# A CIN recommendation tower on one core: group 0 worked in two parts, its rows and every later group's wrapped rows reloaded from DRAM, plain W2 features kept in the rows' memory

## The reference

```python
def _cin_layer(X0, Xi, W, b):            # X0 (512, 39, 16), Xi (512, k, 16)
    Wr = W.reshape(H, 39, Xi.shape[1])   # H = 128
    return einsum('hjk,bjd,bkd->bhd', Wr, X0, Xi) + b[None, :, None]
Xi = X0 = e                              # the gathered rows
for W, b in ((W0, b0), (W1, b1), (W2, b2)):
    Xi = _cin_layer(X0, Xi, W, b)
    res.append(Xi.sum(axis=2))           # z: (512, 3 * 128)
h = concatenate([z, dense_ctx], axis=1)  # (512, 400)
h = maximum(h @ W_top1 + b_top1, 0)      # 512
h = maximum(h @ W_top2 + b_top2, 0)      # 256
y = h @ W_top3                           # (512, 1)
```

## Time and profile before

| | |
|---|---|
| median of 3 runs | 664.6 us (663.94 to 665.81) |
| profiled execution, its own time | 664.95 us |
| its span | 663.1 us |
| mean granted TensorE clock | 0.992 |
| busy: PE, DVE, ACT, POOL | 95%, 82%, 77%, 56% of the span |
| group 0's T starts | 44.9 us |
| group 1's T starts | 79.3 us |
| last T chunk of group 15 | 605.5 us |

### The profile page before, as it was taken

One profiled execution on the slowest core, in us unless ns is written; L12 is line 12 of the kernel. 1 busy time (PEld: TensorE's weight loads), 2 busy tenths in 40 slices (PEclk: granted clock), 3 DMA queues, 4 the chain that ended last, 5 costly groups with the idle time before them and its releaser, 6 DMA issues.

```text
span 663.1 us, 12298 instructions
## 1 busy us (share of the span) xinstructions
PE 633.2 (95%) x2577; PEld 470.6 (71%) x2577; DVE 544.1 (82%) x1526; ACT 510.0 (77%) x1745; POOL 372.6 (56%) x312
## 2 busy tenths in 40 slices
PE   0589999999999999999999999999999999998998
PEld 0247777777777777777777777777777777785574
DVE  0348789888989898989899888989898989899492
ACT  2138878888788878887888888788878887896394
POOL 6888557675657576766756665756575222224000
PEclk9799999999999999999999999999999999999999
DMA  6357687767677787767677767677787765566100
GB/s 226 55 101 162 121 181 147 159 135 161 127 161 140 155 161 155 149 143 145 145 142 144 157 135 162 126 162 133 154 162 155 153 149 129 136 125 208 33 0 1
DMA packets 62138, 91.18 MB, mean 137 GB/s; under 512 B 34695, under 2 KB 38708, under 8 KB 61863
## 3 DMA queue, kind: packets, MB, share of 16 engines
q0 software_dynamic: 14192, 51.02, 43.0%
q1 hardware_dynamic: 47926, 39.95, 21.9%
HBM read 10.69 MB, written 1.28 MB: 18 GB/s over the span
## 4 chain that ended last, share of the span: by engine, by line
PE 87%; POOL 4%; DMA 4%; DVE 2%; issue 1%; SPq 1%; ACT 0%; DVEq 0%; POOLq 0%
PE t_bank L503 21%; PE t_bank L504 20%; PE t_bank L505 20%; PE x_bank L461 8%; PE small_bank L488 5%; POOL emb L371 4%; PE t_bank L571 2%; PE x_bank L457 2%; PE x_bank L456 2%; PE x_bank L459 2%; DMA shared<-rep 1%; DVE prod L806 1%; DMA prod<-in_w 1%; PE t_bank L605 1%; PE t_bank L602 1%
## 5 line engine op out<-in xcount | busy, mean ns | idle before, releaser
L682 ACT ACTIVATE prod<-t_bank,x0t 128x128 f32<-128x128 f32 x1472 | 416.6, 385 | 70.0 <-PE t_bank L505 63.8
L806 DVE SCALAR_TENSOR_TENSOR prod<-t_bank,x0t,prod 128x128 f32<-128x128 f32 x1024 | 286.6, 341 | 49.3 <-PE t_bank L505 48.8
L503 PE MATMUL t_bank<-w_hi,x_hi 128*128 128x512 f32 (+1 forms) x640 | 288.9, 451 | 1.4 <-DVE x_lo L795 1.1
L504 PE MATMUL t_bank<-w_lo,x_hi 128*128 128x512 f32 (+1 forms) x640 | 247.2, 386 | 0.0
L505 PE MATMUL t_bank<-w_hi,x_lo 128*128 128x512 f32 (+1 forms) x640 | 246.7, 385 | 0.0
L371 POOL DMA_INDIRECT emb<-in_table,idx x160 | 215.7, 1348 | 48.5 <-issue 47.9
L381 POOL TENSOR_TENSOR diag<-x0t,mask 128x320 f32<-128x320 f32 x64 | 85.0, 1328 | 182.0 <-PE small_bank L488 104.9
L503 PEld LDWEIGHTS t_bank<-w_hi,x_hi 128*128 128x128 f32 x640 | 120.2, 188 | 46.1 <-issue 16.4
L504 PEld LDWEIGHTS t_bank<-w_lo,x_hi 128*128 128x128 f32 x640 | 120.5, 188 | 37.8 <-issue 14.4
L505 PEld LDWEIGHTS t_bank<-w_hi,x_lo 128*128 128x128 f32 x640 | 120.1, 188 | 23.7
L838 DVE TENSOR_TENSOR prod<-prod 128x768 f32<-128x768 f32 x189 | 113.7, 601 | 0.2
(11 more groups left out here) (104 smaller groups left out, 382.1 us busy)
## 6 DMA issues: line engine op xcount, KB each, us to landing
prod<-prod POOLq DMA_DIRECT2D x63, 768.0 KB, 6.4
shared<-rep SPq DMA_DIRECT2D x96, 234.0 KB
shared<-rep SPq DMA_DIRECT2D x48, 78.0 KB
emb<-in_table,idx POOLq DMA_INDIRECT x160
G<-in_w SPq DMA_DIRECT2D x1, 2496.0 KB
rep<-rep SPq DMA_DIRECT2D x28, 78.0 KB
rep<-emb_scratch SPq DMA_DIRECT2D x20, 78.0 KB
prod<-in_w SPq DMA_DIRECT2D x1, 1536.0 KB, 8.1
```

The lines of the kernel that those rows point to most:

```text
L503: pe.matmul(acc, hi, w1_hi[:, cols], start=True, stop=False)
L504: pe.matmul(acc, hi, w1_lo[:, cols], start=False, stop=False)
L682: last = act.activation(prod[:, s, SLOT[c] + u, :], t_bank[c % T_BANKS][:, u * H:(u + 1) * H], ACT.Copy, scale=x0t[:, s, j:j + 1])
L806: last = dve.scalar_tensor_tensor(unit, t_bank[c % T_BANKS][:, u * H:(u + 1) * H], x0t[:, s, j:j + 1], unit, ALU.mult, ALU.add)
```

## The change

- **Group 0 in two parts** of 256 columns. Each part has its own ids, loaded folded so that 5 gathers of 126 or 124 rows bring it in (`gather_part`); the second part's gathers follow the first's. SP stores and loads each part (`store_part`, `load_part`). Pairs of a part are 256 columns wide, formed in `prod` memory. The even second factors of the first part are issued by ACT, the odd ones by SP. T starts when the first part's x1 is split. The second part's pairs, products and x1 run inside tiles 0 and 1 of group 0's T, at p = 7 to 18.
- **Group 1's pairs** move to late in group 0: DVE forms them at p = 24 to 33, PE multiplies at p = 27 to 36, all seven as plain f32 matmuls with no split; X0 is transposed after p = 20, x1 follows at p = 37 and 38.
- **Gathers.** POOL issues both parts and group 1 before its first diagonal; group 2's ten are issued in group 0, five after the first diagonal and five after the first fold, then nine of group 3.
- **Wrapped rows.** `load_x0` makes all four loads from DRAM for every group; `copy_x0` goes. All four stand between b5 and b6 in `factors`.
- **W1** is loaded and split in four pieces; ACT's second and third splits wait for the first part's gathers. Small loads are spread: some to ACT's queue, four to the end of the loop.
- **Tail.** 31 features are split, 8 plain. The plain ones' W2 columns are loaded in one DMA into `rep`, once group 15's rows have been used. Three plain products stand before the G product of tile 62 and one before that of tile 63.

The core of the diff:

```diff
-SPLIT_J = 30
+SPLIT_J = 31
+W2_LOADS = [(0, SLOTS), (SLOTS, SPLIT_J)]
+W1_PIECES = [(0, 12), (12, 20), (20, 28), (28, F)]
+PART_X0T_AT = 8
+PART_FORM_AT = [7 + b for b in range(BLOCKS)]
+PART_PAIR_AT = [10 + b for b in range(BLOCKS)]
+PART_X1_AT = (1, 7)
+PART_LO_AT = 18
+FIRST_X0T_AT = 20
+FIRST_FORM_AT = [24, 25, 27, 28, 30, 31, 33]
+FIRST_PAIR_AT = [27, 28, 30, 31, 33, 34, 36]
+FIRST_X1_AT = (3, 7)
+FIRST_LO_AT = 38
+FIRST_GATHERS = [(0, 5), (5, 10), (0, 4), (4, 9)]
+FIRST_INDEX_TILE = 2
...
-            def load_x0(g, half, rows):
-
-                sp.wait_ge(emb_stored, (g + 1) * 16)
+            def load_x0(g, half):
+
+                sp.wait_ge(emb_stored, g * 16)
                 src = emb_rows[bass.ds(g * SLOT_ROWS, GROUP_ROWS), :].rearrange("(b f) d -> f b d", f=F)
-                for row in rows:
+                for row in range(0, REP_ROWS, F):
...
-            def copy_x0(g, half):
...
                     if then_x0 and b == LOAD_BEHIND:
-                        load_x0(g + 1, 1 - half, [0])
+                        load_x0(g + 1, 1 - half)
...
+            store_part(0)
+            load_w1(3)
+            load_part(0)
+            factors_of_part(0)
+            store_part(1)
+            load_part(1)
+            factors_of_part(1)
+
+            store_rows(1, 1)
+            load_x0(1, 1)
+            factors(1, 1, then_x0=True)
...
+            sp.wait_ge(x0t_mm, GROUPS)
+            sp.dma_start(w2_plain, w2[:, SPLIT_J * H:F * H]).then_inc(w2_plain_loaded, 16)
...
+            for part in range(PARTS):
+                gather_part(part)
+            pool.wait_ge(ids_loaded, 16 * 2)
+            index(1, 1)
+            for i in range(GATHERS):
+                gather(i, 1)
...
+            def gather_part(part):
+
+                n = FOLDS * PART_SIZE[part]
+                pool.wait_ge(part_ids_loaded[part], 16 * PART_IDS_LOADS)
+                pool.tensor_tensor(part_idx[0:n, part, :], part_ids[0:n, part, :], part_at[0:n, part, :],
+                                   ALU.add).then_inc(part_index_ready, 1)
...
                 i = b // 2
-                if b % 2:
+                if isinstance(g, int) and g == 1:
+                    pe.matmul(x1_bank[:, :], w_sum[:, b, :], pairs_of(b),
+                              start=b == 0, stop=b == BLOCKS - 1).then_inc(pair_mm, 1)
...
-            for loaded in w2_loaded:
-                pe.wait_ge(loaded, 16)
+            pe.wait_ge(w2_plain_loaded, 16)
             early, late = slice(0, EARLY_COLS), slice(EARLY_COLS, B)
-            for j in range(SPLIT_J, SPLIT_J + EARLY_J // 2):
+            for j in range(SPLIT_J, SPLIT_J + EARLY_J - 1):
                 plain_z2(j, early, start=j == SPLIT_J)
...
+            split_w1_hi(0)
+            act.wait_ge(part_gathered[0], 16 * PART_GATHERS)
+            act.dma_start(prod[:, 0, B1_SLOT, :], b1.to_broadcast([P, H])).then_inc(loop_loaded, 16)
+            act.dma_start(mask[:, :], sample_mask).then_inc(loop_loaded, 16)
+            for i in range(1, W1_EARLY):
+                split_w1_hi(i)
...
+            for b in range(2, BLOCKS, 2):
+                act.dma_start(part_second_at(0, b), rep[b:b + PAIRS, 0, part_cols(0)]).then_inc(part_second[b - 1], 16)
+            for s in range(PART_TILES):
+                copy_x0t(0, s, first=True)
+            split_w1_hi(W1_EARLY)
+            part_x1_hi()
```

More of the change, by code:

```diff
@@ L268, in _, with load_part_ids, load_w1 @@
         def _(sp):
+            def load_part_ids(part):
+                begin, n = PART_BEGIN[part], PART_SIZE[part]
+                for fold in range(FOLDS):
+                    sp.dma_start(part_ids[fold * n:(fold + 1) * n, part, :],
+                                 ids[begin:begin + n, fold * PART_GATHERS:(fold + 1) * PART_GATHERS]).then_inc(part_ids_loaded[part], 16)
+            def load_w1(i):
+                cols = slice(W1_PIECES[i][0] * H, W1_PIECES[i][1] * H)
+                sp.dma_start(w1_raw[:, cols], w1[:, cols]).then_inc(w1_loaded[i], 16)
@@ L322, in factors @@
                     if then_x0 and b == LOAD_BEHIND:
-                        load_x0(g + 1, 1 - half, [0])
-            for g in range(2):
-                store_rows(g, g)
-                load_x0(g, g, range(0, REP_ROWS, F))
-                if g == 0:
-                    factors(0, 0)
-            with sp.Fori(1, GROUPS - 2, 2) as odd:
-                for g, half in ((odd, 1), (odd + 1, 0)):
-                    factors(g, half, then_x0=True)
-                    copy_x0(g + 1, 1 - half)
+                        load_x0(g + 1, 1 - half)
@@ new lines, in _ @@
+            store_part(0)
[8 more added lines that the diff above has]
+            factors(1, 1, then_x0=True)
+            with sp.Fori(2, GROUPS - 2, 2) as even:
+                for g, half in ((even, 0), (even + 1, 1)):
+                    factors(g, half, then_x0=True)
+            sp.dma_start(bias[:, 1:2], b2).then_inc(tail_loaded, 16)
@@ L335, in _ @@
+            sp.dma_start(bias[:, 2:2 + M1], top_b1).then_inc(tail_loaded, 16)
+            sp.dma_start(bias[:, 2 + M1:], top_b2).then_inc(tail_loaded, 16)
+            sp.dma_start(w3[:, :], top3).then_inc(tail_loaded, 16)
+            factors(GROUPS - 2, 0, then_x0=True)
             factors(GROUPS - 1, 1)
@@ L409, in group @@
                     t = g * TILES_PER_GROUP + s
-                    if early and s == INDEX_TILE:
+                    if early and s == (FIRST_INDEX_TILE if first else INDEX_TILE):
                         index(g + AHEAD + 1, 1 - half)
@@ L417, in group @@
                         fold((s - 1) % TILES_PER_GROUP)
-                    if gathers and s < INDEX_TILE:
+                    if first:
+                        for i in range(*FIRST_GATHERS[s]):
+                            gather(i, half if s < FIRST_INDEX_TILE else 1 - half)
+                    elif gathers and s < INDEX_TILE:
                         for i in range(GATHERS_EARLY, GATHERS):
                             gather(i, half)
-                    if early and s >= INDEX_TILE:
+                    if early and not first and s >= INDEX_TILE:
                         for i in range(3 * (s - INDEX_TILE), 3 * (s - INDEX_TILE) + 3):
@@ L497, in t_chunk @@
                     pe.wait_ge(x0t_ready, then_x0t * TILES_PER_GROUP)
+                if first_tile and c in W1_CHUNKS:
+                    pe.wait_ge(w_split_lo, W1_CHUNKS.index(c) + 1)
                 if not (first_tile and c < T_BANKS):
@@ L584, in _ @@
             g_multiply(TILES - 1, 2)
-            for j in range(SPLIT_J + EARLY_J // 2 + 1, SPLIT_J + EARLY_J):
-                plain_z2(j, early)
             pe.wait_ge(g_copied, TILES)
```

350 lines of the change are left out of this document (246 added, 104 removed).

## The result

The changed kernel takes 667.99 us (median of 10, 666.7 to 669.6) against 664.76 us for the kernel before (10, 662.4 to 665.8) on the same chip, a ratio of 1.0053 with the interval 1.0038 to 1.0069. It is 3.2 us slower; the forecast was 661.5 and faster. The profiled execution has a span of 667.4 us in place of 663.1, 4.3 more; its own time, 669.23 us, is 1.2 above the median of its ten, so it stands at their slow end.

The account below looks back on a forecast made before the run. PE, 87% of the span, was taken as the bound, with gains only before T, in the first group and in the tail. 664.95 - 1.0 (head) - 2.4 (tail) = 661.55, given as 661.5; own range 659 to 664.5, overall 653.5 to 668.

Parts of the forecast that it names:

- T of group 0: Head: with 5 gathers in place of 10 in the first part, T starts at 31.0, 13.9 us earlier.
- The sum over POOL: POOL in group 0: gathers, index instructions, diagonals, fold and DVE holds add to 59.8; group 2's rows landed at 61.4.
- the held gather: Head: the second part's fourth gather waits on POOL for DVE's W1 split to end, 3.6 us lost.
- rival (a): Group 0: DVE holds no gather, group 2's rows land at 55.8; 656 us, or 652 with quick landings; chance 0.28.
- Later groups: Fourteen groups swap three copies for more reloads; b6 comes about 0.8 us later, cost taken as zero.
- its cover: Later groups: slack before a later b6 costs time, DVE's 1 us and PE's 3.8.
- rival (c): Every later group: b6 lands after PE's use; 0.5 us each is 7 us, total 668.5; chance 0.08.
- The tail: End of kernel: W2's columns already there, tile 62's G product at 613.4, 2.0 earlier; 2.4 us gained in all.
- rival (d): Tail does nothing, say because the clock falls and W2 was not awaited; 664, no change; chance 0.07.
- The last line of the sum: Whole kernel: 664.95 - 1.0 - 2.4 = 661.55 against the profiled execution, 0.35 above the median; stated as 661.5.
- From those rows to group 1: SP's store, reloads and b6 after group 2's gathers: group 1 starts at 78.3, leaving 1.0 of the head's 13.9 us.
- Rival (b): Group 0: store falls behind tile 1's fold, group 1 at 84.1, clock costs 1 to 2 us; 668 us; chance 0.12.

Follow-up runs that it names:

- Experiment 7: Group 0's folds cut to 16 of 128 rows: in the changed kernel 661.85 us; with b5 and b6 also ahead of group 2's store and reload 656.67 us.
- experiment 5: Changed kernel plus eight extra f32 matmuls in PE's idle wait for b6 in group 0: 667.16 us, ratio 1.0036.
- a complete kernel: Changed kernel with b5 and b6 ahead of group 2's store and reload, and one DVE instruction folding 112 rows of group 0's tiles 1 and 2: 658.22 us.
- experiment 9: Kernel before with the tail part alone, plus folds of group 0's tiles 0 and 1 by one DVE instruction for 112 rows: 664.2 us, ratio 0.9997.

## Why the prediction was wrong

**What was right.** T of group 0: 12.9 us earlier, 13.9 forecast. The sum over POOL: group 2's rows stored at 59.92, 61.4 forecast, with the held gather (3.6 lost forecast, 4.41 - 1.28 = 3.1 measured; ten and four pieces of the W1 split show what held it, but not that anything is won without it). The Trainium skill (SBUF — State Buffer, SBUF: two separate sides), read as rival (a) read it, would let a gather's issue run beside such an instruction; the runs say no. But a gather takes its row numbers from `part_idx` or `idx` on chip, and if its issue counts as GpSimd work that reads SBUF, the page and the runs agree; no run here tests that. Rival (a) falls with the rows stored at 59.92. Later groups: zero, 35.43 in the profile of every kernel with a stall-free loop, though the four reloads take 6.5 us of issue there (at 102.70) and b6 goes out at 144.5 in place of 133.53, 3.9 later in its group when the lag of 7.1 is taken off. The forecast priced them at 2.7 of issue and 0.8 of lateness, so it is luck that its cover was enough. With that rival (c) falls for this kernel. The tail: 2.4 forecast, 2.6 measured, with tile 62's G product at 620.29 - 6.87 = 613.42 for a forecast of 613.4, so rival (d) falls. The last line of the sum should have been 661.2: the 0.35 us between the profiled execution and the median was named there and not taken off.

**The step that failed is "From those rows to group 1".** Term by term, forecast and changed kernel:

| term | forecast | measured |
|---|---|---|
| rows of group 2 stored | 61.4 | 59.92 |
| store landed | 3.5 | 7.46 (59.92 to 67.38) |
| four reloads issued | 2.9 | 7.27 (67.38 to 74.65) |
| b6 landed | 5.0 | 3.14 (74.65 to 77.79) |
| formed | 0.7 | 0.69 |
| from there to T of group 1 | 4.8 | 6.47 |
| T of group 1 | 78.3 | 84.95 |

Two terms hold the error, the store with 4.0 and the reloads' issue with 4.4, less 1.9 for b6. I had the store's upper end from the earlier trace rows and went below the middle because the fold is issued at the same moment; it was issued 2.2 us ahead, as it was 1.6 ahead in the kernel before (56.91 and 58.55), and the store took even more than the upper end of 6.6. For the reloads I had only the earlier trace rows, taken when no fold was running, and no upper end at all. Of three steps on one queue, two stood beside folds of 768 KB, and both went past the highest price that the sum had for them. Experiment 7 confirms it: with the folds' data gone the reloads issue in 2.89, just the forecast's price, and T of group 1 starts at 79.77. The 1.5 us above the forecast's 78.3 are there the store (4.8 for 3.5) and the clock (6.4 for 4.8), less rows that are stored 1.9 earlier; b6 lands in 5.4, near the 5.0 of the forecast.

The third error is the clock: 6.47 against 4.8, and group 1 itself lasts 37.03 from T to T in place of 35.59. Rival (b) had named the clock with 1 to 2 us; experiment 5 gives 1.5 up to T and 1.6 behind it, in the traces.

**Rival (b)** is what happened: its mechanism and its place. It put the lateness into the store and b6, though, while half of it was the reloads' issue: b6 landed in 3.14 where it had 7.6, the reloads took 7.27 where it had 2.9, and the two errors cancel. So that its 668 meets the median of 667.99 (the profiled execution, from which it was worked out, has 669.23) is in part luck. It had 0.12. The Trainium skill (DMA: Bandwidth & Descriptors, Specifications) spoke against the short runs. In the loop of the changed kernel they cost no time, since PE never waits for them there; beside a fold the four hold SP's queue for 6.2 to 11.2 us.

**What the change is worth.** Its tail gives 2.6 us and its head costs 7.1 (6.9 by the tail). Four orders of the head gave the same 661.7 to 662.8, about the tail alone: T started 12.9 us sooner, and group 0's folds 5 to 9 us sooner with it, while group 2's rows still came at 60 and met the folds. That the folds' data is what took the gain back was shown by cutting it, and then by a complete kernel at 658.2 us; that the DMA engines as a whole were the limit is my reading of the shares.

## What to carry to other kernels

When an edit starts one stage earlier, list the transfers that start earlier with it and add them up over the stretch where they meet the ones that didn't move; look at the share of the very microseconds in which they meet, since the kernel before had a mean of 0.75 there and still 0.92 beside its store. Price every DMA of a queue on the critical path by a row taken beside the same neighbour, and if there is none take the upper end for all of them together, since one neighbour slows them all. A mend that only changes the order moves the wait; one that takes bytes off the engines, here by using a vector engine with room, removes it, if PE was waiting for them: experiment 9 freed the same kind of transfer and won nothing.

## What the hardware showed that I had not expected

- The issue of a DMA is itself slow beside a fold: four reloads (three of 78 KB and one of 12) took 2.7 to 3.3 us to issue alone, 6.2 to 7.7 beside one fold and 11.2 beside two.
- A few more DVE instructions ahead of a loop can cost 20 us in it. With two instructions more, 12 instruction packets and no stall; with eight to twelve more, waits counted, 42 to 43 packets (0.34 MB in place of 0.10) and six stalls of up to 5.3 us, 28 to 30 us in all. That the packets are DVE's own instructions fetched again is my reading; the rows show only that both come together. Where between these counts it turns was not tried.
- After 7.3 us of idle time PE worked at a granted clock of 0.50 for 3.2 us and at 0.56 once more after a wait of 1.75 us. Behind a wait of 1.84 us it was 0.56 in one kernel and 1.00 in another.
